# Attention sums with the probabilities as stationary operand, normalised on GpSimd, turned by DMA and projected in fp16

## The reference

```
q, k, v = layernorm(x) @ w_q, ctx @ w_k, ctx @ w_v        # 16 heads of 64
out = softmax(q k^T / 8) v, heads side by side
x = x + tanh(g_xattn) * (out @ w_o + b_o)
f = layernorm(x); f = f + selfattention(rmsnorm(f)) @ wo; h2 = rmsnorm(f)
x = x + tanh(g_ffn) * (f + shared(h2) + sum of the top 2 of 8 experts(h2))
```

## Time and profile before

| | |
|---|---|
| median of three runs | 1554.85 us (1554.59 to 1562.48) |
| the profiled execution | 1549.06 us, its span 1547.3 us, granted clock 0.968 |
| busy PE / DVE / ACT / POOL | 1403.9 / 1049.6 / 811.3 / 577.4 us |
| line 751, PE, 128 x 400 fp16, p_hi, c_both | 1536 matmuls, 392.0 us |
| line 430, POOL, 128 x 800 | 128 times, 1906 ns each |
| line 839, PE, 97 x 129 fp32 | 512 instructions, 75.1 us |

### The profile page before, as it was taken

The page is one execution under the profiler, slowest core; times in us unless marked ns, Lnnn a source line. Parts: engine busy times, 40 slices in busy tenths (PEclk is TensorE's granted clock), DMA queues, the critical chain, the costliest instruction groups (busy, mean ns, idle before and its releaser), DMA issues.

```text
span 1547.3 us, 28471 instructions
## 1 busy us (share of the span) xinstructions
PE 1403.9 (91%) x8776; PEld 825.4 (53%) x8776; DVE 1049.6 (68%) x1900; ACT 811.3 (52%) x1188; POOL 577.4 (37%) x699
## 2 busy tenths in 40 slices
PE   4769999999999999999998999999999999888898
PEld 4225555555555464555555555555554645455676
DVE  2778676667675767676766676676767675865765
ACT  1124656465655555455555465656555555454554
POOL 3023433333333434333333343333333342444454
PEclk9579999999999999999999999999999999899999
DMA  7020202020202010020202020202020100000000
GB/s 220 19 55 1 56 1 56 1 57 1 56 1 57 1 36 21 7 51 1 56 1 57 1 56 1 57 1 56 1 57 1 42 1 1 1 1 1 7 7 11
DMA packets 66960, 43.22 MB, mean 28 GB/s; under 512 B 52966, under 2 KB 62410, under 8 KB 66826
## 3 DMA queue, kind: packets, MB, share of 16 engines
q1 hardware_dynamic: 66826, 41.43, 10.6%
HBM read 15.38 MB, written 0.82 MB: 10 GB/s over the span
## 4 chain that ended last, share of the span: by engine, by line
PE 68%; DVE 14%; issue 9%; ACT 4%; POOL 2%; DMA 2%; DVEq 1%; SPq 0%; ACTq 0%; POOLq 0%
PE psum L751 18%; PE psum L812 8%; PE psum L732 8%; PE psum L734 7%; PE psum L736 7%; DVE mx L1237 5%; PE psum L839 4%; PE psum L764 3%; PE psum L803 3%; PE psum L861 3%; PE psum L852 3%; PE psum L777 2%; DVE mx L1271 1%; ACT p_hi L948 1%; DVE y_sb L1259 1%
## 5 line engine op out<-in xcount | busy, mean ns | idle before, releaser
L947 ACT ACTIVATE p<-psum 128x800 f32<-128x800 f32 (+1 forms) x384 | 321.6, 837 | 569.7 <-PE psum L736 567.5
L1237 DVE TENSOR_REDUCE mx<-psum 128x1 f32<-128x512 f32 (+3 forms) x624 | 388.0, 653 | 81.9 <-PE psum L812 78.7
L430 POOL TENSOR_TENSOR p_lo<-p,p_hi 128x800 f16<-128x800 f32 x128 | 243.9, 1906 | 475.5 <-ACT p_hi L948 463.9
L751 PE MATMUL psum<-p_hi,c_both 128*128 128x400 f16 (+1 forms) x1536 | 392.0, 337 | 26.1 <-POOL p_lo L430 16.9
L948 ACT ACTIVATE p_hi<-psum 128x800 f16<-128x800 f32 (+1 forms) x384 | 319.4, 832 | 0.0
L430 DVE TENSOR_TENSOR p_lo<-p,p_hi 128x800 f16<-128x800 f32 (+1 forms) x256 | 260.0, 1016 | 54.7 <-ACT p_hi L948 25.6
L812 PE MATMUL psum<-cT_both,qk_hi 96*128 96x512 f16 (+3 forms) x624 | 236.0, 391 | 61.1 <-DMA cT_both<-c_new 15.6
L751 PEld LDWEIGHTS psum<-p_hi,c_both 128*128 128x128 f16 (+1 forms) x1536 | 143.4, 98 | 155.4 <-issue 38.1
L732 PE MATMUL psum<-qk_hi,cT_both 97*128 97x400 f16 (+1 forms) x768 | 198.2, 340 | 12.0 <-issue 4.8
L734 PE MATMUL psum<-qk_lo,cT_both 96*128 96x400 f16 (+1 forms) x768 | 197.0, 338 | 0.0
L736 PE MATMUL psum<-qk_hi,cT_both 96*128 96x400 f16 (+1 forms) x768 | 196.0, 337 | 0.0
(11 more groups left out here) (181 smaller groups left out, 1730.4 us busy)
## 6 DMA issues: line engine op xcount, KB each, us to landing
c_both<-c_new SPq DMA_DIRECT2D x16, 768.0 KB, 4.9
ctx_nat<-in_ctx_dram SPq DMA_DIRECT2D x16, 528.0 KB
wg<-in_L_ffn_e_gate_dram SPq DMA_DIRECT2D x1, 1024.0 KB, 5.4
wu<-in_L_ffn_e_up_dram SPq DMA_DIRECT2D x1, 1024.0 KB, 7.5
wd<-in_L_ffn_e_down_dram SPq DMA_DIRECT2D x8, 128.0 KB, 4.7
out_dram<-x SPq DMA_DIRECT2D x4, 200.0 KB
x<-in_x_dram SPq DMA_DIRECT2D x1, 600.0 KB
p<-in_L_xattn_w_q_dram SPq DMA_DIRECT2D x1, 512.0 KB, 4.4
```

The costliest lines, as they stand in the source:

```text
L430: engine.tensor_tensor(p_lo[0:m, i % 3, :, :], p32[0:m, i % 3, :, :], p_hi[0:m, i % 3, :, :], ALU.subtract).then_inc(lo_made(b, i)[0], 1)
L751: t = mm(outs[k], w[parity][0:m, j, :], p[0:m, i % 3, k, :], start=(j == 0 and w is c_hi and p is p_hi), stop=(j == CH - 1 and w is c_lo))
L947: a(p32[0:m, i % 3, :, :], src, ACT.Exp, scale=DH ** -0.5)
L1237: v.tensor_reduce(mx[0:r, rt, part:part + 1], bank[0:r, 0:w], AX.X, ALU.max)\
```

## The change

- `pv_unit` swaps the operands: the probabilities are stationary, in tiles of 128 query rows, and the context chunk moves, 97 columns (with the ones) or 96 (the lo half of the context). The halves are cut anew: six tiles (768 rows) and seven tiles (832 rows, padded to 896) instead of 800 and 800. The sums come out as 128 query rows x 97 for each tile.
- `acc_evac` copies them in two instructions into one buffer `acc_sb` (before there were two), and POOL normalises (`normalise`): a reciprocal by a power of -1, a product into an fp16 half, the product again in fp32, and the rest as the other fp16 half, both in `a_new`.
- SP turns `a_new` by two DMA transposes a half (`turn`) into `aT`, the rows of which are the context's width.
- The projection is y1 in unit 6 and y0 in unit 19, one bank each: three passes (hi hi, hi lo, lo hi) for each of 7 or 9 heads, all adding into one 100 x 128 sum in PSUM; `Nh` is kept as two fp16 halves, scaled by 256. DVE adds the result to `x1` in one instruction.
- "ln" to "f" 12, "rs" move by one unit, `norm_1` to unit 7 and `norm_2` to unit 22 of POOL's list; LO_POOL is (5, 7, 9, 11, 13, 16, 18, 20, 22). `h_hi` and `h_lo` use the memory of `c_both[0]` and `cT_both[0]`.

```diff
-    YB = [(0, 1, 2), (3, 4, 5), (6, 7)]
-    YW = D + 1
+    TILES, PER_BANK = (6, 7), (3, 4)
+    WIDE = (6 * P // 2, (ROWS - 6 * P) // 2)
+    ROW0 = (0, 6 * P)
+    PW = 2 * WIDE[1]
+    Y_HEADS = (range(0, 7), range(7, H))
+    Y_SCALE = 256.0
...
-    for n, i in enumerate((2, 3, 4)):
-        plan[i].append(("y1", n))
-    for n, i in enumerate((15, 16, 17)):
-        plan[i].append(("y0", n))
-    plan[6].append(("ln", 0))
-    plan[8].append(("xf", 0))
-    for n, i in enumerate((8, 9, 10, 11, 12, 13, 12, 13, 14, 15, 16, 18, 19, 23)):
+    plan[6].append(("y1", 0))
+    plan[19].append(("y0", 0))
+    plan[7].append(("ln", 0))
+    plan[9].append(("xf", 0))
+    for n, i in enumerate((9, 10, 11, 12, 13, 14, 13, 14, 15, 16, 17, 19, 20, 23)):
         plan[i].append(("f", n))
-    plan[20].append(("rs", 0))
+    plan[21].append(("rs", 0))
     plan[22].append(("h2", 0))
-    CTX_AT, Y0_AT = 0, 18
-    LO_POOL = (6, 8, 10, 12, 14, 16, 18, 20)
+    CTX_AT, NORM1_AT, ACC0_AT, NORM2_AT = 0, 7, 14, 22
+    LO_POOL = (5, 7, 9, 11, 13, 16, 18, 20, 22)
...
+            def turn(b, half):
+                t0, t1 = ROW0[half], ROW0[half] + TILES[half] * P
+                for k in range(2):
+                    wait_apart(sp, acc_norm, (b * 2 + half) * 2 + (k + 1))
+                    sp.dma_start_transpose(aT[:, k, t0:t1].rearrange("p (j k) -> p j k", k=P),
+                                           a_new[:, k, 0:TILES[half], :].rearrange("p j c -> p (j c)")).then_inc(at_in, 16)
...
                     ctx_made(b + 1, 1 - parity)
+                    turn(b - 1, 1)
+                    turn(b, 0)
                     row_of(b, kind, parity)
...
+            def normalise(b, half):
+                n, at = TILES[half], b * 2 + half
+                sums, rc = acc_sb[:, 0:n, 0:C], acc_rc[:, 0:n].unsqueeze(2).broadcast_to([P, n, C])
+                hi, lo = (a_new[:, k, 0:n, 0:C] for k in range(2))
+                pool.wait_ge(acc_out, at + 1)
+                g.tensor_tensor(acc_rc[:, 0:n], acc_sb[:, 0:n, C], minus_one[:, 0:n], ALU.pow).then_inc(acc_rcp, 1)
+                if not (isinstance(b, int) and b == 0 and half == 0):
+                    pool.wait_ge(at_in, at * 32)
+                wait_apart(pool, acc_rcp, at * 2 + 1)
+                g.tensor_tensor(hi, sums, rc, ALU.mult).then_inc(acc_norm, 1)
+                g.tensor_tensor(sums, sums, rc, ALU.mult).then_inc(acc_rcp, 1)
+                pool.wait_ge(acc_norm, at * 2 + 1)
+                wait_apart(pool, acc_rcp, at * 2 + 2)
+                g.tensor_tensor(lo, sums, hi, ALU.subtract).then_inc(acc_norm, 1)
...
                 if kind != "first":
-                    for n in range(len(YB)):
-                        add_heads(b - 1, 1, n, free_of)
-                    norm_1(b - 1)
+                    normalise(b - 1, 1)
                 for i in range(UNITS):
-                    if i == Y0_AT:
-                        if kind == "first":
-                            set_wait(pool, set_dve, SET_DVE, "x1 3")
-                        for n in range(len(YB)):
-                            add_heads(b, 0, n, free_of)
+                    if i == NORM1_AT and kind != "first":
+                        norm_1(b - 1)
+                    if i == ACC0_AT:
+                        normalise(b, 0)
+                    if i == NORM2_AT and kind != "first":
+                        norm_2(b - 1)
...
-                outs = [psum[:, ACCB + k, 0:GW] for k in range(2)]
-                for w, p in ((c_hi, p_hi), (c_hi, p_lo), (c_lo, p_hi)):
-                    for k in range(2):
-                        t = mm(outs[k], w[parity][0:m, j, :], p[0:m, i % 3, k, :],
-                               start=(j == 0 and w is c_hi and p is p_hi), stop=(j == CH - 1 and w is c_lo))
+                half = i // CH
+                for p, c, wide in ((p_hi, c_hi, C + 1), (p_hi, c_lo, C), (p_lo, c_hi, C + 1)):
+                    for n in range(TILES[half]):
+                        bank, k = divmod(n, PER_BANK[half])
+                        t = mm(psum[:, ACCB + bank, k * (C + 1):k * (C + 1) + wide],
+                               p[0:m, i % 3, n * P:(n + 1) * P], c[parity][0:m, j, 0:wide],
+                               start=(j == 0 and k == 0 and c is c_hi and p is p_hi),
+                               stop=(j == CH - 1 and p is p_lo), skip_group_check=True)
...
-                    if n == 0:
-                        pe.wait_ge(acc_out, b * 2 + (half + 1))
-                    for k, h in enumerate(YB[n]):
-                        t = mm(bank[0:S, k * YW:(k + 1) * YW], acc_sb[half][:, h // 4, (h % 4) * S:(h % 4 + 1) * S],
-                               Nh[:, half * HALF + h, :], start=True, stop=True)
+                    heads = Y_HEADS[half]
+                    pe.wait_ge(at_in, (b * 2 + (half + 1)) * 32)
+                    for h in heads:
+                        hi, lo = (aT[0:C, k, h * S:(h + 1) * S] for k in range(2))
+                        for a, w in ((hi, Nh_hi), (hi, Nh_lo), (lo, Nh_hi)):
+                            t = mm(bank[0:S, 0:D], a, w[:, h, :], start=(h == heads[0] and a is hi and w is Nh_hi),
+                                   stop=(h == heads[-1] and a is lo))
...
                 elif kind in ("y0", "y1"):
+                    xb = x1[:, bat(b), :].squeeze(1)
                     dve.wait_ge(aux_free, free)
-                    v.reciprocal(y_rc[:, 0:nh], heads[:, :, D]).then_inc(y_rcp, 1)
...
-                    tt(y_sb[:, at % 2, 0:nh, :], heads[:, :, 0:D],
-                       y_rc[:, 0:nh].unsqueeze(2).broadcast_to([S, nh, D]), ALU.mult).then_inc(aux_free, 1)
+                    stt(xb, bank[0:S, 0:D], 1 / Y_SCALE, xb, ALU.mult, ALU.add).then_inc(aux_free, 1)
```

More of the change, by code:

```diff
@@ L119, in flamingo_kernel @@
     LAST = []
-    for n, unit in enumerate([("y1", 0), ("y1", 1), ("y1", 2), ("ln", 0), ("xf", 0)] + [("f", n) for n in range(13)] +
+    for n, unit in enumerate([("y1", 0), ("ln", 0), ("xf", 0)] + [("f", n) for n in range(13)] +
                              [("rs", 0), ("h2", 0), ("f", 13), ("r", 1)]):
@@ L227, in flamingo_kernel @@
         qk_lo = [sb(f"qk_lo{q}", [C, ROWS], F16) for q in range(2)]
[L228 to L231, removed]
+        p32 = sb("p32", [P, 3, PW])
+        p_hi = sb("p_hi", [P, 3, TILES[1] * P], F16)
+        p_lo = sb("p_lo", [P, 3, TILES[1] * P], F16)
+        acc_sb = sb("acc_sb", [P, TILES[1], C + 1])
+        acc_rc = sb("acc_rc", [P, TILES[1]])
+        minus_one = sb("minus_one", [P, TILES[1]])
+        a_new = sb("a_new", [P, 2, TILES[1], P], F16)
+        aT = sb("aT", [P, 2, sum(TILES) * P], F16)
         mx = sb("mx", [P, RT, MP])
@@ L417, in flamingo_kernel @@
         comb = xlnT[0:S, 3 * B * E:3 * B * E + B * (E + 1)].rearrange("p (b e) -> p b e", e=E + 1)
[L419 to L422, removed]
+        silu = p32[:, :, 0:GW]
+        hidden = p32[:, :, GW:2 * GW]
+        hid_hi, hid_lo = (t[:, :, :].rearrange("p a (k w) -> p (a k) w", k=2)[:, :, 0:GW] for t in (p_hi, p_lo))
         def probs_rest(eng, engine, b, i):
-            m = kc(i % CH)[1]
+            m, w = kc(i % CH)[1], 2 * WIDE[i // CH]
             eng.wait_ge(probs_hi, b * UNITS + (i + 1))
@@ L655, in body @@
                         probs_rest(pool, g, b, i)
-                if kind != "first":
-                    norm_2(b - 1)
             batches(pool, body)
-            def free_at_end(unit):
-                return aux_base(B, "end")[1] + numbered(LAST)[unit][1] + 1
+            normalise(B - 1, 1)
             for kind, n in LAST:
-                if kind == "y1":
-                    add_heads(B - 1, 1, n, free_at_end)
-                elif kind == "ln":
+                if kind == "ln":
                     norm_1(B - 1)
@@ L945, in probs @@
                     act.wait_ge(pv, b * UNITS + (i - 2))
-                src = psum[0:m, 2 * (i % 2):2 * (i % 2) + 2, 0:GW]
-                a(p32[0:m, i % 3, :, :], src, ACT.Exp, scale=DH ** -0.5)
-                a(p_hi[0:m, i % 3, :, :], src, ACT.Exp, scale=DH ** -0.5).then_inc(probs_hi, 1)
+                src = psum[0:m, 2 * (i % 2):2 * (i % 2) + 2, 0:w]
+                to32, to_hi = (t[0:m, i % 3, 0:2 * w].rearrange("p (k w) -> p k w", k=2) for t in (p32, p_hi))
+                a(to32, src, ACT.Exp, scale=DH ** -0.5)
+                a(to_hi, src, ACT.Exp, scale=DH ** -0.5).then_inc(probs_hi, 1)
             def acc_evac(b, half):
                 act.wait_ge(pv, b * UNITS + (half + 1) * CH)
-                a(acc_sb[half][:, :, :], psum[0:C + 1, ACCB:ACCB + 2, 0:GW], ACT.Copy).then_inc(acc_out, 1)
+                if not (isinstance(b, int) and b == 0 and half == 0):
+                    act.wait_ge(acc_norm, (b * 2 + half) * 2)
+                for bank in range(2):
+                    t0, t1 = bank * PER_BANK[half], min(TILES[half], (bank + 1) * PER_BANK[half])
+                    ins = a(acc_sb[:, t0:t1, :], psum[:, ACCB + bank, 0:(t1 - t0) * (C + 1)].rearrange(
```

(2 more changed lines are left out.)

98 lines of the change are left out of this document (42 added, 56 removed).

## The result

The changed kernel takes 1574.5 us (median of four runs, 1563.9 to 1582.5) against 1555.2 before: a ratio of 1.0125, interval 1.0086 to 1.0163. It is slower by 1.3%, where 1490 us and 4% faster had been forecast. Its profiled execution has a span of 1573.8 us at a mean granted clock of 0.934, against 1547.3 and 0.968.

A forecast was written before the change was run, and what follows sets the result against it. PE was taken as the bound, alternating with DVE in the heavy stretch. Savings of 4.7 us a batch over 16 batches, 75 us, less 8 at the end, gave 1554.85 - 67 = 1488, said as 1490 us; range 1450 to 1545.

The forecast's parts named there:

- The pace: Sums (line 751's successor): 97-column matmuls starting 42.9 ns apart, upper bound 55.8; 4.4 us less a batch.
- the light stretch: Units 21 to 3 of a batch, 23.65 us, PE working all the time: 2.4 us a batch saved, all realised.
- Rival 3: Weight loads set the pace of the sums, at 55.8 ns or more: slower, 1576 us; chance 0.10.
- Rival 4: Turned halves land at +14 instead of +10, y1 waits 4.5 us a batch: 1555 to 1565 us; chance 0.08.
- DVE and POOL: Busy time in the whole kernel: DVE down by 70 us, POOL up by about 80, POOL no throughput bound.
- The new chain: Evacuation, POOL's normalisation (6.1 us) and transpose DMA (4.0): y's second-half input is there 10.1 us after the evacuation.
- The wait of y1: Unit 6, PE waiting for the turned second half: 0.5 us a batch, bounds 0 and 3.
- the heavy stretch: Units 4 to 20, with maxima and self-attention, 57.29 us: 70% of 2.8 us realised, 2.0 a batch.
- The prediction's own sign of being wrong: Wrong if the heavy stretch, 57.3 us and forecast at about 54.5, does not shrink; one of three such signs.
- The clock falls in the gap: After PE's 11 us stand at the kernel's end, some us at 1.2 GHz: loss there 13 instead of 8 us.
- The 0.8 us for `y_sb`: PE's waits for y_sb at line 812, 13.8 us in all or 0.8 a batch, go.
- The end: Behind the last batch PE stands 11 us before the last y1, about 3 before: 8 us lost, bounds 5 to 13.

The follow-up runs named there:

- the repaired kernels: Changed kernel and kernel before, each with the loop written out and eight 256-column matmuls filled between the 9-column ones: 1492.3 us and 1529.0 us.
- b_cut4: Kernel before with every 400-column matmul of the sums cut into four of 100, each with its weights: 1602.9 us, ratio 1.032.

## Why the prediction was wrong

**The pace and the light stretch** were right: 43.6 ns against 42.9, and 2.3 us against 2.4. Rival 3 (56 ns) fell: that its 1576 us lie beside the measured 1574.5 is chance. Rival 4 fell too (1.2 us of waiting a batch and not 4.5). The Trainium skill's 81 ns per pair at 128 columns ("TensorE: Matmul & The Clock Gate", "Back-to-back issue gap") does not agree with a second row now, the projection's pairs of 128 columns at 56 ns.

**DVE and POOL** were right in size: 56 us less where 70 was said, 82 more where 80 was said.

**The new chain** was right in its sum, by two errors that cancel. The timeline of POOL in the changed kernel, from the evacuation (ended 668.43) on, and as the last row the one of PE's timeline at which the chain arrives:

```profile
668.51 2.06 POOL L592 TENSOR_TENSOR acc_rc<-acc_sb,minus_one 128x7 f32<-128x7 f32 x1 [10.23 <-ACT acc_sb L971]
670.72 1.32 POOL L596 TENSOR_TENSOR a_new<-acc_sb,acc_rc 128x672 f16<-128x672 f32 x1
672.00 1.30 POOL L597 TENSOR_TENSOR acc_sb<-acc_sb,acc_rc 128x672 f32<-128x672 f32 x1
673.45 1.95 POOL L600 TENSOR_TENSOR a_new<-acc_sb,a_new 128x672 f16<-128x672 f32 x1
...
678.43 0.26 PE L852 MATMUL psum<-Nh_hi,aT 96*100 96x128 f16 x1 [1.08 <-DMA aT<-a_new]
```

10.0 us against 10.1: POOL's part took 7.0 us where 6.1 was said, with a dearer power (2.06 for 1.1), and the transpose landed 2.9 us after its issue where 4.0 was said. The wait of y1 was 1.2 us a batch (27.6 less the end's 9.7, over 15) where 0.5 was taken, within its bounds.

**The step that failed** is the sum's treatment of everything between the instructions: the edit was priced at the durations of its instructions, the jump and the clock inside a batch were put at nothing, and the heavy stretch was to give 70% of its 2.8 us plus 0.8 for waits that go, less 0.5. By the traces the heavy stretches came to 14 us more in all, where 37 less was forecast; the light ones to 1 us less, where 38 less was forecast; the end to 12 us more, where 8 was forecast. The prediction's own sign of being wrong, a heavy stretch that does not shrink, came true. Three terms, of much the same size:

1. The jump back of the loop, some 34 us. It was in the trace of before (1.63 us of "issue" at one jump; the 9% of the chain that the earlier trace rows have under that name are mostly something else, since six jumps make under 10 us) and was taken as a constant. 340 more load-and-matmul pairs a batch, with what else the change brought, made it 7.3 us in place of 1.7. Writing the loop out wins 56 us in the changed kernel and 2 in the one before. The Trainium skill, "Runtime: NRT & Kernel Launch", section "Instruction fetch mechanics", says that instructions are streamed in sequence and that a branch whose target is no longer held has to wait for it to be fetched; the trace agrees in that the stand doubles when PE's matmuls alone are made more and shorter (b_cut4) and is gone without the jump. No row shows a fetch as what ended it.
2. The clock inside the batches, some 27 us. "The clock falls in the gap" was priced only at the end of the kernel. In the heavy stretch PE was at 1.2 GHz for 2.0 us a batch before and for 5.4 in the changed kernel, mostly behind the 9-column matmuls. Filling them takes it to 0.2 and wins 32 us alone.
3. The waits of the heavy stretch, some 27 us. The 0.8 us for `y_sb` did go, but PE's idle time rose from 3.3 to 5.5 us a batch, where the sum had room for 0.5 more. 1.2 us of it is the wait for ACT's `pT`, 1.3 the wait for `aT` (0.5 was taken). ACT had been passed over as no bound because it is busy only 46 of 81 us. The two rows, before and changed:

```profile
PE psum L812 <- ACT pT L995: 12.4, 28, 0.6
```

```profile
PE psum L823 <- ACT pT L1015: 29.3, 42, 0.8
PE psum L852 <- DMA aT<-a_new: 27.6, 15, 9.7
```

The sizes are estimates from the stretches: six jumps at 5.6 us more, and 16 batches at half of 3.4 us more at 1.2 GHz and at 1.7 us of waiting beyond the 0.5. The third is most of what the repairs leave: the repaired kernels are 37 us apart and not 67.

The end was forecast at 8 us of loss and lost 12.4; in the repaired kernels it loses 9.7 (179.4 against 169.7 us from unit 21 of the last batch). PE's stand of 9.7 us was forecast at 11. But PE's time lost in it is not the reason: filling it won nothing. What is left is that the last batch's chain starts late.

## What to carry to other kernels

A trade of few long matmuls for many short ones is paid a second time where PE's program jumps: count PE's instructions in the loop body, read the idle time at the jump in the trace of before, and try the loop written out before judging the change (in the kernel before, with a stand of 1.2 to 1.6 us, that alone won nothing). Look at the granted clock behind every stretch in which PE is busy with few columns, and in all batches: one batch at full clock hid most of the loss here. And judge a shorter engine step by which result it will then be waiting for: an engine that is busy for little more than half of the time can be the one.

The best version, the changed kernel with both repairs, takes 1492 us, 4% less than the kernel before.

## What was not expected of the hardware

- At the loop's jump PE stands for 2.9 to 3.3 us with 14216 or 15688 matmuls in the program, against 1.2 to 1.6 with 8776. In the changed kernel the granted clock is at 1.2 GHz for 6.8 us around each jump.
- Behind a stretch of 2.8 us with PE busy throughout on 32 matmuls of 9 columns the granted clock is often at half; with eight matmuls of 256 columns among them it stays up in 15 of 16 batches, at 0.4 us each (mean clock 0.934 to 0.959 with the loop kept, 0.948 to 0.971 without).
- In the unchanged kernel removing the jump lowered the mean clock (0.968 to 0.947) and ate its own gain.
- A power on GpSimd costs 1.3 to 2.1 us for six or seven elements a partition, at least as much as a product over 672 of them (1.3).
